# A Gram through four pixel buffers, opening mixes through four staging tiles and banks, and a copy that changes its place

## What is computed

```python
def layer0(x, gamma):                       # b, c, n = h*w
    q = x.reshape(b, c, h * w)
    att = einsum('bcn,bdn->bcd', q, q)      # the Gram matrix, 64 x 64 an image
    rev = max(att, axis=-1) - att
    return gamma * einsum('bcd,bdn->bcn', softmax(rev), q) + x
def layer1_and_3(x, hx, hy, bias):          # causal convolution along both axes
    return causal_conv2d(x, outer(hx, hy)) + x * bias
def layer2(x, v, conv_w, tau):              # haar2d, then for p in 0, 1: v * . , 64 x 64 channel product,
    ...                                     # soft threshold by tau; sum and inverse haar2d
```

## Time and profile before

| | us |
|---|---|
| median of three runs | 6386.52 |
| the profiled execution | 6390.89 |
| its span | 6389.1 |
| TensorE busy | 5852.7 (92%) |
| VectorE, ScalarE, GpSimd busy | 3975.6 (62%), 3883.7 (61%), 2526.3 (40%) |
| first Gram, first layer to last chunk | 16.6 to 119.8 |
| first opening mix, matmuls | 135.9 to 277.7 |
| `forward_stage(-1)`, first Toeplitz product to last block product | 286.1 to 675.7 |
| second opening mix, matmuls | 681.6 to 822.7 |

### The profile page before, as it was taken

One profiled execution on the slowest core, in us unless ns is written; L12 is line 12 of the kernel. 1 busy time (PEld: TensorE's weight loads), 2 busy tenths in 40 slices (PEclk: granted clock), 3 DMA queues, 4 the chain that ended last, 5 costly groups with the idle time before them and its releaser, 6 DMA issues.

```text
span 6389.1 us, 154198 instructions
## 1 busy us (share of the span) xinstructions
PE 5852.7 (92%) x47200; PEld 4944.5 (77%) x47200; DVE 3975.6 (62%) x6260; ACT 3883.7 (61%) x6105; POOL 2526.3 (40%) x2436
## 2 busy tenths in 40 slices
PE   5588589999999999999999999999999999999689
PEld 3277268888888888888888888878888887788579
DVE  1033158755886567755786568855786557766866
ACT  0222257755776667755776667755776657755865
POOL 0000045522553245522554245522554235533952
PEclk7599689999999999999999999999999999999789
DMA  6655666576666766666665866667665855534224
GB/s 183 208 179 175 208 191 206 185 238 207 206 207 191 249 186 206 202 214 215 204 207 184 253 191 207 197 215 229 194 206 179 253 173 166 166 116 138 76 85 129
DMA packets 770795, 1216.97 MB, mean 190 GB/s; under 512 B 78854, under 2 KB 475047, under 8 KB 770568
## 3 DMA queue, kind: packets, MB, share of 16 engines
q1 hardware_dynamic: 623112, 945.61, 50.0%
q10 hardware_dynamic: 147456, 268.50, 11.7%
HBM read 808.07 MB, written 405.73 MB: 190 GB/s over the span
## 4 chain that ended last, share of the span: by engine, by line
PE 85%; ACT 4%; DVE 3%; DMA 3%; issue 3%; ACTq 1%; SPq 1%; POOL 1%; DVEq 0%; POOLq 0%
PE ps L467 29%; PE ps L469 14%; PE ps L517 8%; PE ps L485 8%; PE ps L493 7%; PE ps L477 7%; PE ps L445 4%; PE ps L626 4%; PE ps L527 3%; DMA mixed<-x 2%; ACT x L802 1%; DMA pix<-in_x_pix 1%; DVE pix L1046 1%; DVE field L960 1%; ACT ps L847 1%
## 5 line engine op out<-in xcount | busy, mean ns | idle before, releaser
L1078 POOL TENSOR_TENSOR mag<-mag,sgn 128x512 f32<-128x512 f32 x896 | 1037.0, 1158 | 2154.8 <-ACT mag L733 2154.8
L467 PE MATMUL ps<-tab_a,img 128*128 128x256 f32 x4096 | 1288.9, 397 | 108.5 <-ACT mid L759 94.2
L1095 POOL TENSOR_TENSOR split_a<-field,split_a 128x512 fp32r<-128x512 f32 x512 | 650.7, 1271 | 1663.8 <-ACT split_a L785 1663.8
L467 PE MATMUL ps<-tab_b,mid 128*128 128x256 f32 x4096 | 1224.4, 381 | 0.0
L469 PEld LDWEIGHTS ps<-tab_a,img 128*128 128x128 f32 x4096 | 787.1, 192 | 110.1
L469 PEld LDWEIGHTS ps<-tab_b,mid 128*128 128x128 f32 x4096 | 778.9, 190 | 105.5
L467 PEld LDWEIGHTS ps<-tab_a,img 128*128 128x128 f32 x4096 | 663.7, 192 | 197.8 <-ACT mid L759 71.7
L469 PE MATMUL ps<-tab_a,img 128*128 128x128 f32 x4096 | 794.1, 276 | 0.0
L937 DVE TENSOR_TENSOR held<-ps,v_t 128x1024 f32<-128x1024 f32 x448 | 548.5, 1224 | 385.1 <-PE ps L517 385.1
L469 PE MATMUL ps<-tab_b,mid 128*128 128x128 f32 x4096 | 787.5, 274 | 0.0
L952 DVE TENSOR_TENSOR diff<-ps,tau_t 128x1024 f32<-128x1024 f32 x448 | 548.3, 1224 | 299.1 <-ACT ps L724 299.1
(11 more groups left out here) (92 smaller groups left out, 9394.3 us busy)
## 6 DMA issues: line engine op xcount, KB each, us to landing
pix<-in_x_pix SPq DMA_DIRECT2D x256, 512.0 KB, 4.4
mixed<-x ACTq DMA_DIRECT2D x512, 256.0 KB, 3.3
img<-mixed SPq DMA_DIRECT2D x512, 256.0 KB, 3.6
tab_a<-filt SPq DMA_DIRECT2D x1024, 128.0 KB, 3.0
tab_b<-filt SPq DMA_DIRECT2D x1024, 128.0 KB, 3.3
out<-res SPq DMA_DIRECT2D x512, 256.0 KB, 3.1
coef<-res ACTq DMA_DIRECT2D x496, 256.0 KB, 2.4
pix<-in_x_rows SPq DMA_DIRECT2D x128, 512.0 KB, 5.0
```

The costliest lines, as they stand in the source:

```text
L467: nc.tensor.matmul(o_ps, src[:, 0, H * half:H * half + H], tab[:, N - 1::-1], start=True, stop=False)
L1078: nc.gpsimd.tensor_tensor(mag[:, s], mag[:, s], sgn[:, s], ALU.mult).then_inc(c_mult, 1)
L1095: nc.gpsimd.tensor_tensor(split_a[:, 1], src, split_a[:, 0].bitcast(F32), ALU.subtract)\
```

## The change

It has three parts, and none adds or removes arithmetic.

1. The first Gram loads into four buffers in turn: the halves of `pix`, `diff` and `rows`. A chunk may be loaded when the chunk four before it is summed. Later Grams keep two.
2. The opening mixes use banks 6, 7, 4, 5 in turn and four staging tiles, the halves of `x1` and of `mid`, each with a `mixed_out` semaphore. TensorE waits for the copies of the chunk two before, a copy for the store of four copies before. Row chunks 2 and 3 of an opening mix are loaded before the wait for `gram_done`. The later mixes keep their banks, tiles and waits; the counts are adapted.
3. Where no shrinkage runs, which is `forward_stage(-1)` alone, ScalarE's copy into `mid` is issued ahead of the high piece.

```diff
+def mix_bank(inv, m):
+
+    return 6 + m % 2 - (0 if inv else m % 4 // 2 * 2)
...
-        staged = x1[:].rearrange("p a b n -> p a (b n)")
+        staged = [x1[:, 0].rearrange("p b n -> p (b n)"), x1[:, 1].rearrange("p b n -> p (b n)"),
+                  mid[:, 0].rearrange("p b n -> p (b n)"), mid[:, 1].rearrange("p b n -> p (b n)")]
+        pixels = [pix[:, 0], pix[:, 1], diff[:].rearrange("p s (j n) -> p (s j) n", n=2 * C),
+                  rows[:].rearrange("p (j n) -> p j n", n=2 * C)]
...
-        pix_in = [sem("pix_in0"), sem("pix_in1")]
+        pix_in = [sem(f"pix_in{i}") for i in range(4)]
...
-        mixed_out = [sem("mixed_out0"), sem("mixed_out1")]
+        mixed_out = [sem(f"mixed_out{i}") for i in range(4)]
...
-            def load_pix(g, chunk, buf):
-
-                sp.wait_ge(gram_chunk, GCH * g + chunk - 1 + CR)
+            def load_pix(g, chunk, buf, bufs=2):
+
+                sp.wait_ge(gram_chunk, GCH * g + chunk - (bufs - 1) + CR)
...
-                sp.dma_start(xrows[buf], src).then_inc(pix_in[buf], 16)
+                sp.dma_start(pixels[buf].rearrange("p j n -> p (j n)"), src).then_inc(pix_in[buf], 16)
...
-            with sp.Fori(0, GCH // 2) as jj:
-                for buf in range(2):
-                    load_pix(0, 2 * jj + buf, buf)
+            with sp.Fori(0, GCH // 4) as jj:
+                for buf in range(4):
+                    load_pix(0, 4 * jj + buf, buf, 4)
...
                     g = b + 2
+                    if not inv:
+                        for buf in (2, 3):
+                            load_xrows(g, buf, buf)
                     sp.wait_ge(gram_done, g + 1)
...
-                    for buf in range(4):
+                    for buf in range(4 if inv else 2):
                         load_xrows(g, buf, buf)
...
-                        for s in mixed_out:
-                            sp.wait_ge(s, 16 * (32 * (b + 2) + 32) + 16)
+                        for s in mixed_out[0:2]:
+                            sp.wait_ge(s, 16 * 32 * (b + 2) + 16)
...
                     for s in mixed_out:
-                        sp.wait_ge(s, 16 * (32 * (b + 2) + 32) + 16)
+                        sp.wait_ge(s, 16 * 16 * (b + 3) + 16)
...
-                        own = pix[:, buf, j, C * e:C * e + C]
+                        own = pixels[buf][:, j, C * e:C * e + C]
...
-                    gram_part(GCH // 8 * layer + g // 2, g % 2, 0, GP, True).then_inc(gram_chunk, 1)
+                    gram_part(GCH // 16 * layer + g // 4, g % 4, 0, GP, True).then_inc(gram_chunk, 1)
...
-                        uses = (GCH // 2) * (b + 2) + q + e // 2 // 2
+                        uses = (GCH // 2) * (b + 2) - GCH // 4 + q + e // 2 // 2
...
-                        pe.wait_ge(mix_copied, 64 * g + 16 * r + 2 * chunk + CR)
+                        pe.wait_ge(mix_copied, 64 * g + 16 * r + 2 * chunk - (0 if inv else 2) + CR)
...
-                                mm = nc.tensor.matmul(ps[C * half:C * half + C, 6 + s, :], mix_w[C * s:C * s + C, :],
+                                bank = mix_bank(inv, 2 * chunk + s)
+                                mm = nc.tensor.matmul(ps[C * half:C * half + C, bank, :], mix_w[C * s:C * s + C, :],
...
+                    def first_copy():
+                        act.wait_ge(f_mm1, n + 1 + CR)
+                        act.wait_ge(f_mm2, n - 1 + CR)
+                        nc.scalar.activation(mid[:, j % 2], halved(ps[:, 0, :]), ACT.Copy).then_inc(f_mid, 1)
+
                     draining = isinstance(q, int) and q == 16
+                    if fwd and not shrink and on[0]:
+                        first_copy()
                     if fwd and on[2]:
                         act.wait_ge(f_mm3, n - 1 + CR)
                         act.wait_ge(f_mm4, n - 2 + CR)
                         nc.scalar.activation(split_b[:, 0], halved(ps[:, 2, :]), ACT.Copy).then_inc(f_hi, 1)
                     if fwd and on[4] and not draining:
                         store()
-                    if fwd and on[0]:
-                        act.wait_ge(f_mm1, n + 1 + CR)
-                        act.wait_ge(f_mm2, n - 1 + CR)
-                        nc.scalar.activation(mid[:, j % 2], halved(ps[:, 0, :]), ACT.Copy).then_inc(f_mid, 1)
                     if shrink and on[0]:
+                        if fwd:
+                            first_copy()
                         relu(1)
...
                         act.wait_ge(mix_mm, 64 * g + 16 * r + m + 1 + CR)
-                        act.wait_ge(mixed_out[m % 2], 16 * (32 * g + 8 * r + m // 2) + 16)
-                        nc.scalar.activation(staged[:, m % 2], ps[:, 6 + m % 2, :], ACT.Copy).then_inc(mix_copied, 1)
+                        if inv:
+                            act.wait_ge(mixed_out[m % 2], 16 * (32 * (g - 1) + 8 * r + m // 2) + 16)
+                        else:
+                            act.wait_ge(mixed_out[m % 4], 16 * (16 * g + 4 * r + m // 4) + 16)
+                        nc.scalar.activation(staged[m % 2 if inv else m % 4], ps[:, mix_bank(inv, m), :], ACT.Copy)\
+                            .then_inc(mix_copied, 1)
...
-                        act.dma_start(rows_of[:, bass.ds(512 * (8 * r + m // 2), 512)], staged[:, m % 2])\
-                            .then_inc(mixed_out[m % 2], 16)
+                        buf = m % 2 if inv else m % 4
+                        act.dma_start(rows_of[:, bass.ds(512 * (8 * r + m // 2), 512)], staged[buf])\
+                            .then_inc(mixed_out[buf], 16)
```

## The result

| | before | after |
|---|---|---|
| median, us | 6386.89 (6386.07 to 6389.64, 4 runs) | 6191.65 (6187.81 to 6194.41, 4 runs) |
| profiled execution, us | 6390.89 | 6187.81 |
| its span, us | 6389.1 | 6186.0 |

The ratio is 0.9693, with a 95% interval of 0.9676 to 0.9710: 195 us gained, where 184 were forecast and the range allowed for 134.5 to 225.5. The profiled execution of before took 4.0 us more than its median and the one of after 3.8 us less, so the two traces lie 203 us apart and not 195. A difference read from the traces is up to 8 us too large in sum.

What follows compares the result with a forecast made beforehand. TensorE dominates the chain, but each changed stage is held by a round trip with nothing full. Gains of 30 (first Gram), 89 (opening mixes) and 65 (copy into mid) sum to 184, giving 6202.5 us, range 6161.5 to 6250.5.

Steps and rivals of the forecast that it cites:

- The middle between the slow and the fast case: First Gram: gain of 37 us, taken between 28 (matmuls slow throughout, 1.97 us a chunk) and 47 (the fast case).
- the fast case: First Gram with fast matmuls throughout: chunks at 1.5 us, layers at 14.1, first filter store at 67 us, gain 47.
- the prediction's sign: First Gram in the profile after: first filter store issued between 67 and 90 us.
- the price of 6 us: Between first Gram and mix: filter stores beside two more pixel loads, chunk 0 behind chunks 2 and 3, together about 6.
- The fast end of the bounds: First Gram: the larger bound of the gain, 41 us, beside a fast-rate gain of 47.
- The pace of 3.2 us: Opening mixes: time per chunk while loads run, against 4.56 before; gains of 45 and 44 us.
- its two prices: Opening mixes, 1.05 MB of traffic a chunk: 2.78 us at 377 GB/s, or pessimistically 3.35 at 313 GB/s.
- Rival 1: Opening mixes: DMA engines hold them at about today's rate, so they gain only some 15 us; 6276, chance 0.07.
- Rivals 2, 4 and 5: Moving the copy into mid gives only 33 (0.13, shared with smaller mix gain); nothing shows (0.03); slower, above 6399 (0.02).
- rival 5: Forward stage without shrinkage: the copy into mid holds up ScalarE's queue, load round trips pace steps; above 6399, chance 0.02.
- Rival 3: Whole kernel: chunks at 2.7 us and a Gram at the fast rate, 41 + 114 + 72 = 227; 6160 or less, chance 0.07.

## Why the prediction was right, point by point

- **What bounds the kernel.** Each stage was held by a round trip with nothing full: right, shown by the shares of 0.93 and more after, and by each part undone bringing the old start, pace or wait back.
- **Part 1, -30 (bounds -18 and -41): the mechanism was right, the size was not.** It is worth 45 by the undone part and 47.7 by the start of the mix, outside the bounds. Two terms failed. The middle between the slow and the fast case was the wrong choice: the Gram ran as the fast case nearly throughout, and the first filter store came at 64.52, ahead even of the 67 of the fast case, where the prediction's sign was 67 to 90. A layer took 13.1 us where that case had 14.1. The rest of the lead is luck: everything began 1.7 us earlier in this trace (14.94 against 16.61), and the six other kernels with this Gram issue the first store at 67.48 to 69.40, just behind the fast case. And the price of 6 us for the stores beside pixel loads and for chunks 2 and 3 ahead of chunk 0 was 2.0 (23.65 against 21.66 us), 2.4 to 3.3 in the three other kernels with the same loads. The kernels with all rows after the Gram (20.4 and 21.1 us) put the order of the rows at 3 to 4 us, so the stores beside two more pixel loads cost nothing that shows. From 66 to 88 us the DMA engines moved 273 GB/s at a share of 0.95, where before, from 114 to 136 us, it was 212 at 0.90. The fast end of the bounds, 47 - 6 = 41, had the full price in it, and the 45 lies beyond it.
- **Part 2, -89 (bounds -60 and -112): right.** 83 by the undone part, 86 by the traces. The pace of 3.2 us was met: (177.37 - 88.17)/28 = 3.19 in the first mix, (611.32 - 524.29)/28 = 3.11 in the second. The last chunks took 2.7 us, not 2.4: (185.41 - 177.37)/3. Of its two prices the scaled one, 3.35 us (the share scaled up to full, 313 GB/s), was nearer than the 2.78 of the best 8 us of the trace (377 GB/s): the mixes ran at a share of 0.96 and 0.98 with 321 and 337 GB/s. That the chosen 3.2 was met to 0.1 us is partly luck, since it was picked between the two and not worked out. One sign was missed: TensorE's waits on the copies were to be gone, and half of them stayed, 39.3 us, with ScalarE's waits on stores (23.6 and 10.3 us) behind them.
- The Trainium skill's 358 GB/s for HBM transfers ("SBUF — State Buffer", "Summary: rules for kernel authors") would have made it 2.93 us. The mixes reached 321 and 337 GB/s, so the rule lies 12% and 6% above what stretches of 4 KB reads and 2 KB writes gave here.
- **Part 3, -65 (bounds -58 and -72): right.** 67 by the undone part and by the traces. The step is 4.79 us; the forecast said 4.87 less 0.1 for overlapping weight loads, which no row priced. The 0.08 is there: from the Gram's half chunk to the first Toeplitz product it is 306.99 - 306.38 = 0.61 us, where it was 412.03 - 410.26 - 1.08 = 0.69. Nothing took the wait's place: 0.6 us to spare on the low piece, 220 GB/s instead of 175.
- **Rival 1** (the DMA engines hold the mixes at about today's rate) was wrong about the rate, but it named the limit that the mixes did reach. The page "TensorE: Matmul & The Clock Gate" of the Trainium skill ("HAM oscillation — how this bites in real kernels"), which tells of a kernel that PSUM double-buffering didn't help, fits this case in part: four banks beside two tiles gave 26 of the 83 us, which is more than nothing and a third of what banks and tiles give together.
- **Rivals 2, 4 and 5** didn't come. In rival 5 the loads of the first Toeplitz product would have had to take over 7.6 us; `img` lands in 4.0 us and `tab_a` in 3.2 (medians, 220 to 500 us).
- **Rival 3** (better than the sum) was right for the Gram, 45 against its 41, and wrong for the mixes.
- **The sum.** 184 forecast, 195 measured: part 1 short by 15, part 2 long by 6, part 3 short by 2. That part 1 and part 2 missed in opposite directions brought the sum nearer, and that is luck.

## What to carry to other kernels

Where a stage is a round trip and no resource is full, count the links of the trip and widen all of them at once: here banks alone gave 26 us and staging tiles alone 19, both together 83. Then price the result by the next full resource, with the rate of a long stretch scaled to a full share rather than with the best few microseconds; in this case that was 3.35 and 2.78 us a chunk, and 3.1 to 3.2 came. And in a program written by hand for each engine, look for the instruction that is ready early and queued late: moving one copy ahead of another copy and a store took 67 us from 64 steps, and nothing in the trace got slower by it.

## What the runs showed that I had not expected

More work made a stage faster: 64 matmuls of zeros in the first Gram brought its first filter store from 114.19 to 102.45 us, because the real matmuls ran at 1.15 instead of 1.97 us a chunk, with a granted clock of 1.00 instead of 0.69 (30 to 100 us). It was one execution. And moving 3 MB of stores out of the way of a stage that is bound by transfers moved its start by 12.4 us and its end by 3 us, which the five runs can't tell from nothing.
